# The last layer norm of each tile: from one VectorE operation to ScalarE, with a bias from GpSimd

## What is computed

```python
x = _layernorm(x + attention(x))                 # 16 heads of 128, causal, ALiBi, RMS norms of q, k, y
x = _layernorm(x + cross_mix(x, ctx))            # softmax(query key^T) mixes the channels
x = _layernorm(x + bitlinear_ffn(x))             # quantised weights and activations, sigmoid gate
def _layernorm(x, axis=-1, eps=1e-05):
    m = jnp.mean(x, axis=axis, keepdims=True)
    v = jnp.var(x, axis=axis, keepdims=True)
    return (x - m) / jnp.sqrt(v + eps)
```

## Time and profile before

| what | value |
|---|---|
| median of 3 runs | 434.47 us |
| lowest and highest | 434.25 and 435.78 us |
| span of the profiled execution | 432.9 us |
| time of the profiled execution outside its span | not given; the median is 1.57 us above the span |
| busy in the span: TensorE, VectorE, ScalarE, GpSimd | 401.9, 327.7, 254.4, 220.2 us |
| chain that ended last: TensorE, VectorE, ScalarE, GpSimd | 86%, 5%, 4%, 1% |

### The profile page before, as it was taken

One profiled execution on the slowest core, in us unless ns is written; L12 is line 12 of the kernel. 1 busy time (PEld: TensorE's weight loads), 2 busy tenths in 40 slices (PEclk: granted clock), 3 DMA queues, 4 the chain that ended last, 5 costly groups with the idle time before them and its releaser, 6 DMA issues.

```text
span 432.9 us, 9595 instructions
## 1 busy us (share of the span) xinstructions
PE 401.9 (93%) x2605; PEld 361.1 (83%) x2612; DVE 327.7 (76%) x1000; ACT 254.4 (59%) x750; POOL 220.2 (51%) x368
## 2 busy tenths in 40 slices
PE   4979999999999999999999999999999899999552
PEld 3668899999999999999999999999988677777321
DVE  0777987887797798788779779878822788888862
ACT  3486777677676776767767677676722333333321
POOL 3633667676675776767767677675501122222210
PEclk9999999999999999999999999999999999999965
DMA  8980010110101101011010110000000000000000
GB/s 223 316 251 2 2 36 3 38 37 0 36 0 36 36 0 36 0 36 36 0 36 0 36 36 0 0 0 0 0 2 0 2 0 15 12 14 12 13 14 24
DMA packets 21747, 14.52 MB, mean 34 GB/s; under 512 B 1760, under 2 KB 21472, under 8 KB 21728
## 3 DMA queue, kind: packets, MB, share of 16 engines
q1 hardware_dynamic: 21728, 14.29, 11.2%
HBM read 13.24 MB, written 1.05 MB: 33 GB/s over the span
## 4 chain that ended last, share of the span: by engine, by line
PE 86%; DVE 5%; ACT 4%; issue 2%; DMA 1%; POOL 1%; SPq 0%; POOLq 0%; DVEq 0%
PE ps L482 30%; PE ps L422 11%; PE ps L493 7%; PE ps L506 6%; PE ps L499 5%; PE ps L512 4%; PE ps L505 3%; PE ps L514 3%; PE ps L513 3%; PE ps L521 3%; PE ps L587 3%; PE ps L572 2%; ACT hT L696 2%; DMA x_sb<-in_x 1%; PE ps L557 1%
## 5 line engine op out<-in xcount | busy, mean ns | idle before, releaser
L315 POOL TENSOR_TENSOR qk_rstd<-qk_sum,minus_half 128x2 f32<-128x2 f32 x128 | 88.5, 692 | 92.6 <-DVE qk_sum L797 90.8
L482 PE MATMUL ps<-w_hi,xT_hi 128*128 128x384 f32 x256 | 96.9, 378 | 2.3 <-DVE qk_n L791 1.4
L482 PE MATMUL ps<-w_hi,xT_lo 128*128 128x384 f32 x256 | 86.5, 338 | 0.0
L482 PE MATMUL ps<-w_lo,xT_hi 128*128 128x384 f32 x256 | 86.3, 337 | 0.0
L797 DVE TENSOR_REDUCE qk_sum<-sq 128x2 f32<-128x258 f32 x128 | 53.6, 419 | 30.8 <-ACT sq L635 29.1
L635 ACT ACTIVATE sq<-ps 128x256 f32<-128x256 f32 x128 | 49.1, 384 | 34.6 <-PE ps L482 34.4
L791 DVE TENSOR_TENSOR qk_n<-ps,qk_rstd 128x256 f32<-128x256 f32 x128 | 54.2, 423 | 18.8 <-POOL qk_rstd L315 17.8
L422 PE MATMUL ps<-wp,yT 128*128 128x256 f32 x256 | 62.2, 382 | 0.0
L310 POOL TENSOR_TENSOR y_rstd<-y_sum,minus_half 128x2 f32<-128x2 f32 x64 | 49.0, 766 | 24.6 <-DVE y_sum L804 20.9
L673 ACT ACTIVATE sqy<-ps 128x258 f32<-128x258 f32 x64 | 24.8, 387 | 58.5 <-PE ps L514 58.5
L422 PEld LDWEIGHTS ps<-wp,yT 128*128 128x128 f32 x256 | 46.7, 190 | 5.9
(11 more groups left out here) (126 smaller groups left out, 846.9 us busy)
## 6 DMA issues: line engine op xcount, KB each, us to landing
w_raw<-in_L_attn_Wq SPq DMA_DIRECT2D x16, 128.0 KB, 2.2
w_raw<-in_L_attn_Wk SPq DMA_DIRECT2D x16, 128.0 KB, 2.3
w_raw<-in_L_attn_Wv SPq DMA_DIRECT2D x16, 128.0 KB, 2.3
wp<-in_L_attn_Wproj SPq DMA_DIRECT2D x1, 2048.0 KB, 16.1
ff_raw<-in_L_ffn_w_gate SPq DMA_DIRECT2D x1, 1024.0 KB, 8.6
ff_raw<-in_L_ffn_w_up SPq DMA_DIRECT2D x1, 1024.0 KB, 11.0
ff_raw<-in_L_ffn_w_down SPq DMA_DIRECT2D x1, 1024.0 KB, 13.0
out<-fin SPq DMA_DIRECT2D x8, 128.0 KB, 1.7
```

The source lines that it names most:

```text
L315: pool.tensor_tensor(qk_rstd[:, t, :], qk_sum[:, t, :], minus_half[:], ALU.pow).then_inc(s_rs[t], 1)
L482: last = pe.matmul(ps[:, t, 0:3 * D], xa[:, k, tok], wa[:, r, k * 3 * D:(k + 1) * 3 * D], start=(i == 0), stop=(i == len(parts) - 1))
```

## The change

VectorE's `finish(u)` is taken out. GpSimd makes a new tile `shift`, -mean * rstd, in one operation behind `rstd(2, m - 1)`. ScalarE applies the norm as fin = Identity(rstd * res + shift), at the head of the next turn ahead of its x1T copy, and for the last tile after the loop. The waits go along: for the store of two tiles before on ScalarE; for `ln_rstd` and for the fin before on GpSimd; for shift on ScalarE. VectorE's wait `s_ln[2] >= u` ahead of L908 stays.

```diff
+        shift = sb("shift", [P, 1])
...
+        s_shift = sem("last_shift_set")
...
                 if m > 0:
                     rstd(2, m - 1)
+                    pool.wait_ge(s_lnr[2], m)
+                    wait(pool, s_ln[2], m - 1)
+                    pool.tensor_scalar(shift[:], mean_var[:, 2, 0:1], ln_rstd[:, 2:3], -1.0, ALU.mult,
+                                       ALU.mult).then_inc(s_shift, 1)
...
+            def finish(u):
+                wait(act, s_out[u % 2], 16 * (u // 2))
+                act.wait_ge(s_shift, u + 1)
+                act.activation(fin[:, u % 2], res[:, 2], ACT.Identity, scale=ln_rstd[:, 2:3],
+                               bias=shift[:]).then_inc(s_ln[2], 1)
+
             for m in range(NT + 1):
                 u = m - 1
+                if m > 1:
+                    finish(u - 1)
                 if m < NT:
                     act.wait_ge(s_t1, m + 1)
...
+            finish(NT - 1)
...
-            def finish(u):
-                wait(dve, s_out[u % 2], 16 * (u // 2))
-                normed(2, u, fin[:, u % 2])
-
...
-                if m > 1:
-                    finish(u - 1)
...
-            finish(NT - 1)
```

## The result

The changed kernel takes 436.89 us (median of 6 runs, 436.76 to 437.15) beside 434.68 us (median of 6) for the kernel before: ratio 1.0047, 95% interval 1.0032 to 1.0061. The kernel became slower in both, by 0.47% and by 0.31%. Forecast were 435.1 us, and 434.0 to 436.7 as the range.

A forecast was written before the change was run, and what follows sets the result against it. TensorE was taken to bound the loop; 0.1 us (filled tiles) + 0.09 (m = 7) + 0.46 (end) = +0.65 us on the profiled span, 432.9 to 433.55, plus 1.57 to the median: 435.1 us, range 434.0 to 436.7.

The forecast's parts named there:

- What bounds the loop: Tile loop: TensorE bounds it at 11.0 us a tile, VectorE less than 0.1 us behind in every second tile.
- the first rival: GpSimd's shift costs 0.54 us, x1 and hq come 0.44 us late, TensorE waits: 437.1 us; chance 0.10.
- What fin's removal gives: Filled tiles: freeing VectorE of 0.41 us gives nothing directly, as x waits for ln_rstd; ln_rstd gets 0.04 us shorter.
- the third rival: GpSimd comes free 0.20 us earlier without fin, the pauses at L577 go in three tiles: 434.8 us; chance 0.10.
- What it adds on GpSimd: After ln_rstd: hand-over 0.08 us, shift 0.19, so the next first-norm var_eps and x1 come 0.09 us late.
- The margin behind it: Between hq and its transposes: 0.13 us left in one kind of tile, 0.21 in the other, covering the 0.09 delay.
- filled tiles: Tiles m = 2 to 6: xq 0.05 us late in three of five, 0.1 us in all, 0 to 0.15.
- The end: After the last ln_rstd: shift and its hand-over added, fin 0.60 us instead of 0.41; +0.46 us, 0.36 to 0.84.
- the dear shift: Same as the first rival: shift at 0.54 us on GpSimd becomes the wait, +2.6 us to 437.1 us; chance 0.10.
- VectorE as the bound: Rival in the tile loop: VectorE sets tile time, each filled tile wins 0.45 us, giving 432.8 us; chance 0.08.
- hq behind var_eps: Other route to the third rival: hq moves behind var_eps's start, 0.10 us apart, freeing GpSimd earlier; 434.8 us.
- The clock at another place: Rival in the last two tiles: one L572 matmul group changes clock level, 435.1 us less or plus 0.84; chance 0.07.

The follow-up runs named there:

- three kernels with shift out of the way: Changed kernel without shift (ratio 1.0011); with shift made behind the next tile's first ln_rstd (1.0014); the latter with the last tile's norm on VectorE (1.0002).
- tile-only kernel: The kernel before with only the tile shift and its semaphore declared, used by nobody; ratio 1.0002.
- two shifts: The changed kernel with GpSimd making shift twice, one behind the other into two tiles; ratio to the kernel before 1.0089.
- shift later: The changed kernel with shift made behind the next tile's first ln_rstd and the norm applied behind ScalarE's x1T copy; ratio to the kernel before 1.0014.
- changed, again: The changed kernel's same code measured a second time, on another chip: 436.26 us beside 434.47 us, ratio 1.0031.

## Why the prediction was right and wrong

**What bounds the loop** was read rightly: TensorE, with VectorE and its waits close behind. The wait that takes the place is the one that the first rival names, at a smaller price.

**What fin's removal gives** was read as nearly nothing, and it is little. Half of the 0.41 us became idle time. The second norm comes 0.10 us sooner after hq where the forecast had 0.04, and with that the waits for xq go, which the forecast priced at 0.08 us in three turns. The three kernels with shift out of the way have a loop 0.23 to 0.24 us shorter. That is the gain of the third rival in size, without the cost that cancels it; its mechanism did not come about, since ln_rstd became 0.03 to 0.04 us shorter without fin, not 0.20. It is hq that holds GpSimd up: ln_rstd lasts 0.93 us beside it in the changed kernel, 0.55 alone.

**The step that failed is the delay of x1 in "What it adds on GpSimd".** It said: a hand-over of 0.08 us, shift of 0.19, var_eps starting where shift ends, 0.09 us late. The runs showed a hand-over of 0.10 (374.10 to 374.20), a shift of 0.26 (the pointer adds 0.07) and a gap of 0.08 us between shift and var_eps that I had put at nothing. The sum is 0.44 us instead of 0.27, and with the 0.17 us that GpSimd had been idle there taken off, 0.28 us instead of 0.09 (each by its rows).

The margin behind it was read well: 0.13 us in one kind of turn and 0.21 in the other, where the runs show 0.11 of delay covered against the loop without shift. With 0.28 us put into the same reckoning, three filled turns pay 0.15 and two 0.07, 0.59 us; the trace has 0.69. So the term "filled tiles" was 0.1 for want of 0.19 us in the delay, of which 0.15 and 0.07 lie above the margin. Its path was another one too: the 0.1 us was put on a later xq, but in the changed kernel the wait for xq is gone, and TensorE waits for hq, which the forecast held to be covered. In turn 7, where the delay is paid whole, the forecast had 0.09 and the trace 0.25.

**The end** was forecast as +0.46 us and measured as +0.54. fin on ScalarE is 0.60 us, as worked out from L694 less 768 columns. The page "ScalarE: Activation LUTs" of the Trainium skill, section "What ACT_TABLE_LOAD costs", gives 186 ns, 93 ns for each pointer operand and 0.833 ns per column, an estimate of 585 ns here; the trace agrees, with 599 ns as the median. The rest of the miss is again shift's 0.26 and its hand-over.

**The sum**: 0.65 us forecast, 1.46 us by the traces of loop and end. On the 434.47 us that the forecast started from, 1.46 us give 435.9 us, inside the range; the first median of 436.89 us is outside it. Of the 1.0 us between, 0.2 is the base, as the median of before is 434.68 us with six runs, and some 0.75 us is in neither loop nor end. In the profiled execution this is a late start; for the other five runs it stays open. The forecast had no term for either. The top of the range was too low for a cost and a late start together. It does not follow from its reason either: half way from 435.1 to the dear shift's 437.1 is 436.1, not 436.7. In the same way the low end of the forecast alone, 434.7, is not the sum of its near ends: 0, 0.09 and 0.36 us give 434.9.

**The dear shift as a rival** had the mechanism, the place and the point from which TensorE pays; its price of 0.44 us of delay was too high, against 0.28. "Slower by over 0.5%" did not come about in either measurement (1.0047 and 1.0031), though the interval of the first reaches above it. **VectorE as the bound** fell: freed of fin and without shift, the filled turn is 0.04 us shorter, not 0.45. **hq behind var_eps** did happen: in the changed kernel var_eps starts at 379.45, 0.10 us ahead of hq, and lasts 0.19 us instead of 0.64; but ln_rstd then lasts 0.93 beside hq, and hq itself had become the wait. The wait where fin stood is therefore 0.44 us, and not the 0.9 that the forecast named as its sign. **The clock at another place** moves the last turns of several kernels here, also of the kernel before's own code: with the tile alone added, the up matmuls of turn 7 ran at the lower level (granted clock 0.50 from 419.7 to 421.2 us), where they had run at the higher one in the first trace (1.00 from 418.4 to 419.1 us). Both rows are from the timeline, the tile-only kernel first:

```profile
419.54 1.91 PE L589 MATMUL ps<-wuT,xqT 128*128 128x512 bf16 x4
```

```profile
418.21 1.03 PE L587 MATMUL ps<-wuT,xqT 128*128 128x512 bf16 x4
```

The two kernels have the same instructions, so this comes with the execution and needs no change of the code; in the two profiles of the changed kernel these matmuls last 1.03 us, as before.

## What to carry to other kernels

An engine that is busy for a quarter of the time (2.77 of 11 us) can still be the link that every tile's chain goes through: before putting work on it, look at what stands behind the new operation in its list, and count the hand-over, the operation and the gap to the next one. If the result is not needed soon, the same operation behind the next tile's first norm costs nothing in the loop: that is the difference between 11.08 and 10.91 us here (fin was moved on ScalarE too, but without shift it was free in its first place). And an operation that ends inside a wait of its own engine is worth little to remove, 0.04 us a turn here, while its slower copy on another engine is paid in full at the end, where nothing runs beside it.

## What the runs showed of the hardware that was not expected

A GpSimd multiply on 128x1 lasts 0.190 us with constants and 0.264 us with one scalar by pointer. The gap behind it is there or not by what comes before: two shifts in a row start 0.24 us apart with none; ln_rstd and a shift whose waits had long been met follow with none (375.34 to 375.33, shift later); but behind a shift that had itself just been released, var_eps came 0.08 us after its end, although its mean_var had been ready for 0.2 us or more. Why is open; it was not tried further.

The loop begins anywhere from 327.6 to 330.0 us in these profiles, whichever the kernel. In the changed kernel's first profile the clock was at its lower level from 24 to 26 us, in that of before it was not; the rows are of the stretch 24 to 26 us (PE, PEld, VectorE, ScalarE, GpSimd busy, then PEclk), the changed kernel first:

```profile
24.00:26.00 2.00, 2.00 (x9) 2.00 (x9) 0.58 (x2) 0.74 (x2) 0.69 (x1) 0.50 1.10 349
```

```profile
24.00:26.00 2.00, 1.50 (x10) 1.44 (x11) 1.16 (x4) 1.25 (x4) 0.69 (x1) 1.00 1.10 349
```

A granted clock of 0.50 is 1.2 GHz of 2.4. TensorE had worked 1.92 us of the 4 us before that, against 2.53 us in the other. But what made it fall is not shown: "changed, again" lost the clock with 2.28 us of work in that stretch, and "two shifts" kept it with 2.05. Nor is the lower clock shown to be the cause of the late start. "Changed, again" had it as well and began its loop at 328.10 us, earlier than the kernel before:

```profile
24.00:26.00 2.00, 2.00 (x8) 2.00 (x8) 0.43 (x1) 0.73 (x2) 0.14 (x1) 0.50 1.10 347
```

And the three profiles with a begin near 329.9 us had the full clock there. Where the late start comes from stays open. With a scatter of 3.6 us between the spans of one kernel, a change of 1.5 us is read from the loop's own instructions, not from the medians of six runs.
